# Gather passes of a four-layer graph network: rounds written out, arrivals signalled by fours, and fewer waits per step

## The reference

```python
def _L0_gnn_ref(feat, src, dst, edge_weight, eps):
    messages = feat[src] * edge_weight[:, None]
    neigh = jax.ops.segment_sum(messages, dst, num_segments=feat.shape[0])
    return (1.0 + eps) * feat + neigh
# L1: edge_weight = sum(z * edge_attr, axis=1), then three times:
    m = h @ conv_weight[i]
    msg = edge_weight[:, None] * m[src]
    agg = jax.ops.segment_sum(msg, dst, num_segments=n_nodes)
    h = _gru_cell(agg, h, w_ih, w_hh, b_ih, b_hh)
# L2: one of 16 relations' projections of each source row, scaled by an attention value
    srcs = alphas[rels] * srcs_dense[rels, src]
    vrps = vrps.at[dst].add(srcs)
    vrps = vrps.at[dst].add((vfts @ update)[dst])
# L3: mean over neighbours in the other direction
    agg = segment_sum(x[col], row) / maximum(deg, 1)
    return (x + agg) @ W.T + b
```

## Time and profile before

| | |
|---|---|
| timed, median of 3 | 6613.13 us |
| profiled execution: span | 8247.0 us |
| GpSimd busy | 4812.8 us (58%) |
| VectorE busy | 3797.9 us (46%) |
| TensorE busy, matmuls | 3559.9 us (43%) |
| gathers of ring tiles | 4702 |
| steps | 5000 (two matmul records each) |

### The profile page before, as it was taken

One profiled execution on the slowest core, in us unless ns is written; L12 is line 12 of the kernel. 1 busy time (PEld: TensorE's weight loads), 2 busy tenths in 40 slices (PEclk: granted clock), 3 DMA queues, 4 the chain that ended last, 5 costly groups with the idle time before them and its releaser, 6 DMA issues. The chain is left out here.

```text
span 8247.0 us, 87733 instructions
## 1 busy us (share of the span) xinstructions
PE 3559.9 (43%) x13560; PEld 2744.4 (33%) x13561; DVE 3797.9 (46%) x13361; ACT 861.3 (10%) x2167; POOL 4812.8 (58%) x5078
## 2 busy tenths in 40 slices
PE   2433334334335444444545444585333334333334
PEld 2333223323234344444334443332322223222233
DVE  4555555555556444444445554433343334233334
ACT  1000001000000111111211110033222222000000
POOL 4666664466663466666356666554656665566664
PEclk5555555555556766666755666687555556555556
DMA  4332332122221111111011111143111111111111
GB/s 107 89 83 81 85 85 65 49 60 60 60 60 46 41 45 45 45 45 44 24 38 45 45 46 45 30 148 139 41 39 44 43 44 42 40 44 44 45 45 45
DMA packets 259358, 467.68 MB, mean 57 GB/s; under 512 B 91601, under 2 KB 164530, under 8 KB 252835
## 3 DMA queue, kind: packets, MB, share of 16 engines
q0 software_dynamic: 158480, 310.78, 15.3%
q10 hardware_dynamic: 35040, 73.87, 2.9%
q1 hardware_dynamic: 65587, 80.28, 2.8%
HBM read 389.31 MB, written 77.27 MB: 57 GB/s over the span
## 5 line engine op out<-in xcount | busy, mean ns | idle before, releaser
L592 POOL DMA_INDIRECT G<-h_rows,ix_src x3920 | 3746.0, 956 | 2469.6 <-issue 1075.5
L695 PE MATMUL ps<-G,M 128*128 x10000 | 2739.2, 425 | 4244.2 <-issue 2834.0
L695 PEld LDWEIGHTS ps<-G,M 128*128 128x128 f32 x10000 | 2189.7, 295 | 4740.3 <-issue 4705.1
L1156 DVE TENSOR_TENSOR HNA<-HNA,ps 128x128 f32 (+1 forms) x3328 | 956.1, 287 | 2118.2 <-remote 1094.3
L1136 DVE TENSOR_SCALAR M<-irow,rel,w_l 128x128 f32<-128x128 f32 x3328 | 1191.7, 360 | 395.4 <-issue 359.7
L592 POOL DMA_INDIRECT G<-t_rows,pos x782 | 747.8, 956 | 495.2 <-issue 212.8
L1156 DVE TENSOR_TENSOR HTA<-HTA,ps 128x129 f32 x840 | 243.9, 290 | 744.4 <-remote 336.7
L695 PE MATMUL ps<-sorting 128*128 128x128 f32 x1568 | 443.1, 379 | 38.1 <-issue 24.6
L1720 ACT ACTIVATE sorting<-sorting,pk 128x128 f32<-128x128 f32 x784 | 250.6, 390 | 1880.8 <-DVE sorting L1333 1139.2
L1156 DVE TENSOR_TENSOR X<-X,ps 128x128 f32 x832 | 239.3, 288 | 378.4 <-issue 221.2
L1792 ACT ACTIVATE G<-G,pk 128x128 f32<-128x128 f32 x782 | 314.0, 402 | 917.6 <-DMA G<-t_rows,pos 857.5
(11 more groups left out here) (261 smaller groups left out, 2124.9 us busy)
## 6 DMA issues: line engine op xcount, KB each, us to landing
G<-h_rows,ix_src POOLq DMA_INDIRECT x3920
t_rows<-G SPq DMA_DIRECT2D x49, 1024.0 KB
HTA<-in_edge_attr_n ACTq DMA_DIRECT2D x50, 500.0 KB
HTA<-in_edge_attr ACTq DMA_DIRECT2D x50, 500.0 KB
sorting<-q_flat ACTq DMA_DIRECT2D x98, 196.0 KB
G<-t_rows,pos POOLq DMA_INDIRECT x782
h_rows<-HNA SPq DMA_DIRECT2D x24, 256.0 KB
h_rows<-HG SPq DMA_DIRECT2D x24, 256.0 KB
```

The source lines that it names most:

```text
L592: return nc.gpsimd.indirect_dma_start(to, None, table, bass.IndirectOffsetOnAxis(ap=ix, axis=0))
L695: return nc.tensor.matmul(dst, lhsT, rhs, start=start, stop=stop, skip_group_check=True)
L1156: V.tensor_tensor(to, to, ps[:, u % SLOTS, 0:n], ALU.add).then_inc(s_add, 1)
```

## The change

The rounds of all passes are written out on TensorE and VectorE (SyncE and ScalarE keep their loops). The 32 semaphores `s_g` become eight, `s_quad`, one for each four gathers in flight; a wait on one is for all four of them (16 counts each). TensorE no longer waits for a step's one-hot, but once a pass for the first four (`lead_built`), and VectorE signals only those. In a step of VectorE the destination's address is worked out by an instruction of its own (`V.lower_ap`) that holds the wait for the matmul, and the add holds the wait for the add before.

```diff
-        s_g = [sem(f"s_g{u}") for u in range(RD)]
+        s_quad = [sem(f"s_quad{j}") for j in range(RD // QUAD)]
-        def rounds(eng, r0, r1):
-            return nullcontext(r0) if r1 == r0 + 1 else eng.Fori(r0, r1)
-        def uses(u):
-            return -(-(EF - u) // RD)
+        def landed(k, j, rounds):
+            before_k = k * sum(16 * min(QUAD, EF - t) for t in range(j * QUAD, EF, RD))
+            return before_k + 16 * QUAD * rounds
             def arrivals(k, tiles, fetched):
-                def one(r, u):
-                    sp.wait_ge(s_g[u], 16 * (k * uses(u) + r + 1))
-                    sp.sem_inc(s_arr[k], 1)
                 with sp.Fori(0, FEED) as r:
-                    for u in range(RD):
-                        one(r, u)
-                for u in range(tiles - FEED * RD):
-                    if FEED * RD + u < fetched:
-                        one(FEED, u)
-                    else:
-                        sp.sem_inc(s_arr[k], 1)
+                    for j in range(RD // QUAD):
+                        sp.wait_ge(s_quad[j], landed(k, j, r + 1))
+                        sp.sem_inc(s_arr[k], QUAD)
+                for t in range(FEED * RD, tiles, QUAD):
+                    j = t // QUAD % (RD // QUAD)
+                    sp.wait_ge(s_quad[j], landed(k, j, FEED) + 16 * min(QUAD, fetched - t))
+                    sp.sem_inc(s_arr[k], QUAD)
...
-                    gather(...).then_inc(s_g[t % RD], 16)
+                    gather(...).then_inc(s_quad[t // QUAD % (RD // QUAD)], 16)
...
                     pe.wait_ge(s_add, k * S + s + 1)
-                    pe.wait_ge(s_m, k * S + s + 1)
...
+            def lead_built(k):
+                pe.wait_ge(s_m, k + 1)
+
             def gather_pass(k, r0, r1, n, extra=None):
-                with rounds(pe, r0, min(r1, FEED)) as r:
-                    one_round(k, r, n, extra)
-                for r in range(max(r0, FEED), r1):
+                if r0 == 0:
+                    lead_built(k)
+                for r in range(r0, r1):
                     one_round(k, r, n, extra)
...
-                ins.then_inc(s_m, 1)
+                return ins
             def lead_in(k, of, weight):
                 for s in range(LEAD):
-                    build(k, s, s, of, weight)
+                    ins = build(k, s, s, of, weight)
+                ins.then_inc(s_m, 1)
...
+                    to = acc[:, bass.ds(at_b[u], 1), 0:n].rearrange("p t d -> p (t d)")
                     dve.wait_ge(s_mm, k * S + s + 1)
+                    V.lower_ap(to)
                     dve.wait_ge(s_add, SLOTS + k * S + s)
-                    to = acc[:, bass.ds(at_b[u], 1), 0:n].rearrange("p t d -> p (t d)")
                     V.tensor_tensor(to, to, ps[:, u % SLOTS, 0:n], ALU.add).then_inc(s_add, 1)
...
-            with dve.Fori(0, FULL3) as r:
+            for r in range(FULL3):
                 one_round(PASS_L3, r, RD, acc3, W1, rel3, None, b3_i)
...
-                    act.wait_ge(s_g[u % RD], 16 * (PASS_L2 * uses(u % RD) + i * (RING // RD) + u // RD + 1))
+                    if u % QUAD == 0:
+                        j = u // QUAD % (RD // QUAD)
+                        got = landed(PASS_L2, j, i * (RING // RD) + u // RD)
+                        act.wait_ge(s_quad[j], got + 16 * min(QUAD, n - u))
                     A.mul(G[:, u, 0:D], G[:, u, 0:D], a_l[:, bass.ds(i * RING + u, 1)])
```

More of the change, by code:

```diff
@@ L1 @@
-from contextlib import ExitStack, nullcontext
+from contextlib import ExitStack
 import concourse.bass as bass
@@ L601, in gather_pass @@
                         pool.wait_ge(s_mm, k * S + t + 3 - RING + BLK)
-                    gather(G[:, t % RING, 0:D], table, ix[:, t:t + 1]).then_inc(s_g[t % RD], 16)
+                    gather(G[:, t % RING, 0:D], table, ix[:, t:t + 1]).then_inc(s_quad[t // QUAD % (RD // QUAD)], 16)
             def deviation(phase, i):
@@ L857, in ordered_half @@
             def ordered_half(k, h, i):
+                if h == 0:
+                    lead_built(k)
                 for rr in range(HALF):
@@ L1160, in gather_pass @@
             def gather_pass(k, r0, r1, acc, n, of, weight, blocks, extra=None):
-                with rounds(dve, r0, min(r1, FEED)) as r:
-                    one_round(k, r, RD, acc, n, of, weight, blocks, extra)
-                for r in range(max(r0, FEED), r1):
+                for r in range(r0, r1):
                     one_round(k, r, RD if r < NRD - 1 else RD - LEAD, acc, n, of, weight, blocks, extra)
```

## The result

The changed kernel takes 6682.69 us (median of 4 runs, 6671.16 to 6686.42); the kernel before, beside it on the same chip, 6613.95 (4 runs, 6611.73 to 6614.97). The ratio is 1.0106, 95% interval 1.0093 to 1.0118: slower by 1.1%, some 69 us. The forecast was no change, 6610 us, and 6682.69 lies outside its range of 6578 to 6635.

The account below looks back on a forecast made before the run. GpSimd's gathers, issued back to back every 1.25 us, were taken to bound the kernel, covering everything else in a pass. Terms 0 + 0 - 2 - 3 + 2 = -3 us on 6613 gave 6610 us, range 6578 to 6635.

Parts of the forecast that it names:

- VectorE's two waits on the address operation and the add: VectorE's step: a 0.02 us instruction less between build and add, under cover, at most 1 us at the six pass ends.
- Gathers back to back: Timed runs: GpSimd issues a gather every 1.25 us and hardly waits for the steps; the rest is under its cover.
- rebuilt sum of 6674: Timed run rebuilt from the trace: 5870 us of gather intervals + 1024 - 262 + 42, against 6613 measured.
- Recording as the cause of 8247 us: Profiled execution: backed-up records make each instruction take 0.70 us to get away, so the span is 1634 us longer.
- slow steps of 4.9 us: Profile after: TensorE's slow steps take 4.9 us instead of 5.6, as one record is gone.
- Loops: Passes written out on TensorE and VectorE: 1 to 4 us a round saved, all under cover, taken as 0.
- fours: One semaphore for four gathers: tiles count as landed up to 3.75 us later; 0 to +6 us, taken as +2.
- One-hot: One wait less per TensorE step: 255 us of sequencer time on no path, 0, or 2 us at the passes' ends.
- lead-in's: Wait for the first one-hots, now on TensorE's first table load of a pass: 0, or 26 us if exposed.
- the 126: Microseconds that written-out passes would save over four looped passes, 32 a pass, if the gathers' cover were gone.
- first rival: Timed runs stall too, steps hold the gathers: gain 32 to 126 us, likeliest 6570 us; chance 0.16.
- The second: Rival: coarser arrival and later start put TensorE behind the ring at gathers 64 to about 80; at most 48 us slower; chance 0.09.

Follow-up runs that it names:

- 6: Run 4's kernel plus one more wait ahead, on a one-hot built long before, so the sequencer again has two operations before an add: 6669.55 us, ratio 1.0088.
- 4: Kernel before with only VectorE's two waits changed, the matmul's on a separate address operation and the previous add's on the add: 6696.43 us, ratio 1.0106.
- the second profile of before: The kernel before, unchanged, profiled once more; that execution was timed at 6608.45 us.
- 5: The changed kernel with VectorE's two waits put back as before, both ahead of the address operation: 6619.28 us, ratio 1.0015.
- 8: Run 4's kernel with the second input of the first pass's edge products read from PSUM instead of SBUF: 6643.51 us, ratio 1.0052.
- 9: Run 4's kernel plus a wait for the add just issued ahead of each group of four products or comparisons: 6626.40 us, ratio 1.0020.
- 10: Run 4's kernel with the products spread one to a step and the comparisons one, two and one to a step: 6626.25 us, ratio 1.0023.
- 7: Run 4's kernel with the two waits swapped, address operation waiting for the previous add and the add for its matmul: 6635.17 us, ratio 1.0036.
- 11: The changed kernel with VectorE's waits as in the kernel before and the products and comparisons spread over the steps: 6613.07 us, ratio 1.0001.

## Why the prediction was wrong

**The step that failed** is "VectorE's two waits on the address operation and the add: ... The same cover, and at the six ends at most 1 us". The effect named there, a sequencer instruction less per step, isn't what cost time (6). The cost measured is 70 us where the term was at most 1 (4), and it lies in what the term left out: GpSimd's gathers take longer beside VectorE's operations. I asked only which engine waits for which semaphore. By that question GpSimd is independent of VectorE until the ring is full, and it is: it waits no longer than before. But GpSimd's own 0.94 us was taken as a constant, and it depends on what VectorE runs beside it. The sign that this isn't constant stood in the earlier trace rows: the longest gather is 1565, 1330, 2187 and 1406 ns in the passes with side work and 1030 in the last, which has none. I read the medians (944, in pass 5 952) and left the third number out.

**Gathers back to back: right.** GpSimd's idle time before gathers is 1578 us in both profiles, and the ordinary interval is 0.94 + 0.30. Put down to TensorE are 80.5 us in 264 pieces of 0.30 each, the ordinary interval under another name:

```profile
POOL G L586 <- issue: 1346.4, 4418, 0.3
...
POOL G L586 <- PE ps L689: 80.5, 264, 0.3
```

**The rebuilt sum of 6674 was near by accident.** It put 5870 us on the passes; the second profile of before has 5923.7 from first to last starts, because of 54 us of lengthening and longer gathers in pass 5. It put 804 us outside them; there are 682.9. Two errors of opposite sign, 54 us too little and 121 too much, came out 1% high. That was luck.

**Recording as the cause of 8247 us: half right at most.** That the slow steps weren't the timed kernel's was right, and the 0.70 us per instruction aren't in the second profile. But it wasn't the number of records, since as many cost nothing there; that they back up and throttle an engine is shown by no run. What slowed that one execution stays open. With it went the tests that I built on it: the slow steps of 4.9 us don't exist in the profile after, and the span fell by 1562 us, not by 300 to 900.

**Loops and fours: right. One-hot: wrong in sign.** The first two were taken at 0 and +2 us and measured at ratios 1.0001 and 0.9997. The one-hot's wait was taken at -2 with the lead-in's at 0, and the two together measured +8 us (1.0004 to 1.0022), which stays unexplained. The adds of a burst lie 0.45 us apart instead of 0.50, as said. The forecast's sum has a term of -3 that no part gives: the parts give 0, -2, -1 at most, +2 and 0. And 35 us isn't a quarter of the 126 (32 is), so the range's lower end takes in a little more of the first rival than it says. Neither changes the outcome.

**The rivals.** The first (steps hold the gathers, faster) is ruled out by the loops alone, ratio 1.0001. The second had the sign, not the mechanism: its place was the ring at gathers 64 to 80, and no gather waits longer than the ordinary 0.31 us there. The mechanism that acted was in none of them, and its 69 us are more than the 48 that the second allowed at most.

**Shown and open.** Shown: the loss is in the VectorE part (4, 5); it is in GpSimd's gather instructions, four fifths of it beside groups of four VectorE operations; for the products, it is their second SBUF input that does it (8); most of it goes when such a group starts behind a wait or isn't a group (9, 10). Supported, not shown: that how far ahead the sequencer has handed instructions to VectorE decides whether GpSimd gets in between two of them. The 0.04 and 0.07 us of the kernels where it does, the 0.02 after the start in 9, and the 0.23 and 0.24 of those where it doesn't, fit. But in the written-out kernels, the changed one among them, no register operation marks the point, and 9 changes the gap before the first product as well (7 doesn't: 0.20 us, as in the part alone). Open: why the comparisons hold half of the gathers and the products nearly all; why gathers beside one-hot builds take longer with this part, which is most of what 9 still has over before; and the 8 us of the one-hot's wait.

## What to carry to other kernels

Where one engine's instruction stream is the pace, check the longest durations of its own instructions, pass by pass, and what the other engines run beside them, not only its waits. On an engine off the path, moving a wait can cost time, though that engine does the same work and nobody waits for it longer: here it shut another engine out for four instructions instead of one. That the instructions close up isn't the reason by itself, since with the swap (7) they do and two thirds of the loss are gone. Where a group of VectorE operations with two SBUF inputs runs beside a stream of GpSimd gathers and holds them to its end, put one of them in each step, or a wait ahead of the group; with the waits of the kernel before, where the gathers get in between anyway, spreading gained nothing over that kernel (11).

## What the runs showed of the hardware

- A gather's 944 ns on GpSimd become up to 2149 ns in the changed kernel when it starts beside four VectorE operations in a row with two SBUF inputs (0.42 us each, 1.42 together). It ends 0.82 us after the operation that held it. With the second input in PSUM the same row of operations costs it nothing (0.94 to 0.95). The Trainium skill (SBUF — State Buffer, section "Who interferes with whom") says that a VectorE instruction with two SBUF inputs contends with a GpSimd instruction that reads SBUF; the traces agree, if the gather counts as one. By the same page of the Trainium skill (section "SBUF: two separate sides") the one that started first has the shared port pair for the whole instruction. That fits before, where gathers get in at the end of one product; it doesn't tell of the changed kernel, where they get in only behind the fourth.
- It takes less than two SBUF tensors to lengthen a gather a little: beside three operations in a row that read one tensor and a column of scalars (line 1183, 0.35 us each) it takes 1.07 us, in 40 cases of the changed kernel's first pass between 1.06 and 1.13.
- The same operations in the same order hold a gather until the next of them ends or until all four have, by where the waits of the *preceding* step stand: held to the end are 0 of 33 before, 6 of 35 with the swap, 25 of 26 in the changed kernel (beside its comparisons 57 of 121, before 1 of 114).
- The load falls one way here: VectorE's four products take 1.42 us whether a gather is held or not.
- One profiled execution of a program spanned 8247.0 us and another of the same program 6606.6. A profile whose span isn't that of the timed runs should be taken again before it is argued from.
